# Attention and routed experts on one core: normalising two slots behind a batch's scores, turning and product three, ScalarE's copies ahead of its exponentials

## The reference

```python
def xattn(x, latents):             # 128 batches, 64 rows of 128 each
    xn, ln = _layernorm(x, gamma_m, beta_m), _layernorm(latents, gamma_l, beta_l)
    q = (ln @ Wq + bq) * DH ** -0.5            # 8 heads of 128
    k, v = split(concat([xn, ln], 1) @ Wkv + bkv)
    out = softmax(q @ k.T) @ v                 # per head, 64 x 128 scores
    return out @ Wo + bo
def ffn(x):                        # 8 experts, the best 2 of each row
    probs = softmax(x @ Wr + br)
    cw = probs where among its row's top 2, else 0
    h = relu(x @ W1[e] + b1[e])                # 128 -> 256
    return sum_e cw[e] * (h @ W2[e] + b2[e])   # 256 -> 128
x = x + tanh(g_xattn) * xattn(ctx, _layernorm(x))
x = x + tanh(g_ffn) * ffn(_layernorm(x))
```

## Time and profile before

| | us |
|---|---|
| runs | 794.71, 795.09, 797.86 |
| median | 795.09 |
| profiled execution, its own time | 800.09 |
| its span, first to last instruction | 798.37 |
| first scores (batch 0) | 29.13 |
| last scores (batch 127) | 681.25 |

### The profile page before, as it was taken

One profiled execution on the slowest core, in us unless ns is written; L12 is line 12 of the kernel. 1 busy time (PEld: TensorE's weight loads), 2 busy tenths in 40 slices (PEclk: granted clock), 3 DMA queues, 4 the chain that ended last, 5 costly groups with the idle time before them and its releaser, 6 DMA issues.

```text
span 798.4 us, 17460 instructions
## 1 busy us (share of the span) xinstructions
PE 761.3 (95%) x5392; PEld 645.5 (81%) x5392; DVE 525.9 (66%) x1829; ACT 497.8 (62%) x1630; POOL 443.1 (55%) x455
## 2 busy tenths in 40 slices
PE   7999999999999999999999999999999999879788
PEld 7778777777888988788988788988878889768665
DVE  4636677685857567677658777767768556465536
ACT  3677767676866566766556576656568655445622
POOL 2233264646552444785656686565668465466663
PEclk9999999999999999999999999999999999999999
DMA  6745151542455542174654146575316456534523
GB/s 196 199 161 193 59 210 71 210 145 81 145 186 158 200 153 71 41 231 160 214 195 146 47 109 219 189 230 172 104 44 199 146 191 205 162 107 122 149 77 87
DMA packets 119791, 119.42 MB, mean 150 GB/s; under 512 B 14585, under 2 KB 94994, under 8 KB 119698
## 3 DMA queue, kind: packets, MB, share of 16 engines
q1 hardware_dynamic: 111088, 102.41, 39.0%
q0 software_dynamic: 7680, 15.74, 6.7%
q10 hardware_dynamic: 930, 0.15, 0.1%
HBM read 35.94 MB, written 41.55 MB: 97 GB/s over the span
## 4 chain that ended last, share of the span: by engine, by line
PE 79%; DVE 6%; issue 6%; ACT 4%; POOL 2%; another core or an unknown queue 2%; DMA 1%; SPq 1%; ACTq 0%; DVEq 0%; POOLq 0%
PE shared L1426 14%; PE batch L1364 12%; PE batch L1377 12%; PE hid_ps L1294 8%; PE xy_ps L1308 7%; PE batch L1372 6%; PE shared L1217 3%; PE shared L1219 3%; PE shared L1218 3%; PE batch L1308 2%; ACT probs L746 2%; PE xy_ps L1271 2%; PE batch L1354 1%; PE shared L1415 1%
## 5 line engine op out<-in xcount | busy, mean ns | idle before, releaser
L676 POOL TENSOR_TENSOR probs<-probs,rsums 128x512 f32<-128x512 f32 x128 | 132.9, 1038 | 234.3 <-DVE rsums L1147 232.0
L746 ACT ACTIVATE probs<-batch,neg_max 128x128 f32<-128x128 f32 x512 | 180.5, 374 | 2.0 <-DVE neg_max L1151 2.0
L651 POOL DMA_INDIRECT sorted_x<-xn,row_of x120 | 121.3, 1011 | 36.0 <-issue 28.0
L827 ACT ACTIVATE qT<-shared,tb 128x512 f32<-128x512 f32 x128 | 87.2, 696 | 85.4 <-PE shared L1219 75.8
L1377 PE MATMUL batch<-pT_sb,kvn 128*128 128x512 f32 x256 | 134.2, 606 | 5.5 <-ACT pT_sb L754 5.4
L1364 PE MATMUL batch<-kvT,qT 128*128 128x128 f32 x1024 | 135.4, 275 | 0.8 <-ACT qT L827 0.8
L1426 PE MATMUL shared<-M,oT 128*128 128x128 f32 x1024 | 125.3, 275 | 0.2
L1364 PEld LDWEIGHTS batch<-kvT,qT 128*128 128x128 f32 x1024 | 124.4, 192 | 1.2 <-ACT qT L827 1.2
L1426 PEld LDWEIGHTS shared<-M,oT 128*128 128x128 f32 x1024 | 119.5, 192 | 1.3 <-issue 1.3
L746 ACT ACTIVATION_READ_ACCUMULATOR probs<-batch,neg_max 128x1 f32 x512 | 110.3, 215 | 0.0
L761 ACT ACTIVATE oT<-batch 128x512 f32<-128x512 f32 x128 | 76.2, 595 | 47.6 <-PE batch L1377 42.6
(11 more groups left out here) (168 smaller groups left out, 1241.7 us busy)
## 6 DMA issues: line engine op xcount, KB each, us to landing
wt<-wall SPq DMA_DIRECT2D x124, 321.0 KB
sorted_x<-yg SPq DMA_DIRECT2D x36, 512.0 KB, 4.9
xt<-sorted_x SPq DMA_DIRECT2D x162, 64.0 KB
sorted_y<-y_sb SPq DMA_DIRECT2D x78, 128.0 KB
kv<-in_ctx_dram SPq DMA_DIRECT2D x16, 256.0 KB
kv<-in_x_dram SPq DMA_DIRECT2D x16, 256.0 KB
xres<-in_x_dram SPq DMA_DIRECT2D x32, 128.0 KB
out_dram<-x SPq DMA_DIRECT2D x15, 256.0 KB
```

Of the source, the lines that this page charges most:

```text
L651: nc.gpsimd.indirect_dma_start(xs[k % SETS][:, :], bass.IndirectOffsetOnAxis(ap=row_of[:, g, choice, c:c + 1], axis=0), xn[:, g % 2, c, :] ...
L676: nc.gpsimd.tensor_tensor(pv, pv, rsums[:, m % 2, :].unsqueeze(2).broadcast_to([P, 4, P]), ALU.mult).then_inc(probs_ready, 1)
L746: last = nc.scalar.activation(probs[:, m % 2, c * P:(c + 1) * P], batch_ps[m % BANKS][:, c * P:(c + 1) * P], ACT.Exp, bias=neg_max[:, m % ...
L827: nc.scalar.activation(qT[:, g % 2, :, number, :], sh[:, :].rearrange("p (b i) -> p b i", b=GB), ACT.Identity, bias=tb[:, number:number + ...
```

## The change

The reciprocal and the multiply of batch m move from slot m + 1 to m + 2 (`REST`), turning and the product from m + 2 to m + 3. ScalarE copies the turned probabilities ahead of the slot's exponentials and no longer behind them. Turning and product go into the bank that the scores of batch m + 1 had (`later_ps`), so that turning also waits for that batch's exponentials, and scores wait for the copy of batch m - 5 instead of m - 4. On TensorE scores come ahead of turning, but for the first slot of a group. What hangs on a group's products, or is numbered like it, comes one slot later: the projection, the second layer norm, routing, scatters, gathers, tiles, the dense expert, and also the load and the layer norm of the next group's rows and their turning. The queries keep their last slot, so that they lie in slots 4 to 7 instead of 3 to 7. `TAIL` becomes 132. The diff shows two of the nine VectorE steps whose slot number goes up by one; the others, and the router's exponential on ScalarE (6 to 7), change in the same way. No instruction on data is added or taken away.

```diff
-LOAD = -15
-STATS = (-12, -12)
-AGGREGATE = -11
-NORMALISE = (-9, -9, -8, -8)
+LOAD = -14
+STATS = (-11, -11)
+AGGREGATE = -10
+NORMALISE = (-8, -8, -7, -7)
...
-EXP, TURN, OUT = 1, 2, 2
+EXP, REST, TURN, OUT = 1, 2, 3, 3
...
-SCATTER = (2, 3, 4, 6)
+SCATTER = (3, 4, 5, 7)
...
-HOMES = 4
-
-MEASURE = {7:(0,1),1:(2,),2:(3,)}
+HOMES = 5
+
+MEASURE = {0: (0, 1), 2: (2,), 3: (3,)}
...
-        n = max(n, GB * (LAST_GROUP[k] + 2) + 7 + AHEAD)
+        n = max(n, GB * (LAST_GROUP[k] + 2) + 8 + AHEAD)
...
-GATHERS = {0: 2, 1: 2, 5: 2, 7: 2}
+GATHERS = {0: 2, 1: 2, 2: 2, 6: 2}
...
-BIAS_SLOT = GB * (G + 1) + 2
+BIAS_SLOT = GB * (G + 1) + 3
 
 SHARED = {
-    0: [("project", -1, 2, "a"), ("place", -2, 0, "c")],
-    1: [("turn_kv", 1, 0, "a"), ("turn_kv", 1, 1, "b")],
-    2: [("project", -1, 3, "a"), ("table", -2, 0, "c")],
-    3: [("query", 1, 0, "a"), ("query", 1, 1, "b")],
-    4: [("project", 0, 0, "a"), ("turn_x", -1, 0, "b"), ("query", 1, 2, "c")],
-    5: [("router", -1, 0, "a"), ("query", 1, 3, "b"), ("query", 1, 4, "c")],
-    6: [("project", 0, 1, "a"), ("query", 1, 5, "b")],
-    7: [("query", 1, 6, "a"), ("query", 1, 7, "b")],
+    1: [("project", -1, 2, "a"), ("turn_kv", 1, 0, "b"), ("place", -2, 0, "c")],
+    2: [("turn_kv", 1, 1, "a")],
+    3: [("project", -1, 3, "a"), ("table", -2, 0, "c")],
+    4: [("query", 1, 0, "a"), ("query", 1, 1, "b"), ("query", 1, 2, "c")],
+    5: [("project", 0, 0, "a"), ("turn_x", -1, 0, "b"), ("query", 1, 3, "c")],
+    6: [("router", -1, 0, "a"), ("query", 1, 4, "b"), ("query", 1, 5, "c")],
+    7: [("project", 0, 1, "a"), ("query", 1, 6, "b"), ("query", 1, 7, "b")],
 }
...
+        def later_ps(m):
+
+            return batch_ps[(m + 1) % BANKS]
+
...
@@ def _(sp)
-                    g = (n + 1 - 4 * half) // GB
-                    if s == (7, 3)[half] and 0 <= g < G:
+                    g = n // GB
+                    if s == (0, 4)[half] and 0 <= g < G:
...
@@ def _(pool)
-                m = n - EXP
+                m = n - REST
...
-                    if s == (1, 7)[half] and 0 <= g < G:
+                    if s == (2, 7)[half] and 0 <= g < G:
...
-                if s == 2 and 0 <= g < G:
+                if s == 3 and 0 <= g < G:
...
@@ def _(act)
-                nc.scalar.activation(pT_sb[:, :], batch_ps[m % BANKS][:, :], ACT.Copy).then_inc(pT_done, 1)
+                nc.scalar.activation(pT_sb[:, :], later_ps(m)[:, :], ACT.Copy).then_inc(pT_done, 1)
...
             def slot(n):
                 if 0 <= n - OUT - 1 < B:
                     keep_product(n - OUT - 1)
+                if 0 <= n - TURN < B:
+                    keep_turned(n - TURN)
                 if 0 <= n - EXP < B:
                     exponentials(n - EXP)
-                if 0 <= n - TURN < B:
-                    keep_turned(n - TURN)
...
@@ def read_logits(n, s)
-                if s == 5 and 0 <= g < G:
+                if s == 6 and 0 <= g < G:
...
@@ def _(pe)
-                wait(pe, o_out, m - BANKS + 1)
+                wait(pe, o_out, m - BANKS)
...
             def turn_probs(m):
                 pe.wait_ge(probs_ready, m + 1)
+                if m + 1 < B:
+                    pe.wait_ge(exp_done, m + 2)
+                else:
+                    pe.wait_ge(o_out, m - BANKS + 1)
                 for c in range(4):
-                    last = nc.tensor.transpose(batch_ps[m % BANKS][:, c * P:(c + 1) * P], probs[:, m % 2, c * P:(c + 1) * P], ident[:, :])
+                    last = nc.tensor.transpose(later_ps(m)[:, c * P:(c + 1) * P], probs[:, m % 2, c * P:(c + 1) * P], ident[:, :])
...
             def slot(n):
                 if n >= TAIL and n + 1 in TILE_AT:
                     turn_tile(TILE_AT[n + 1])
+                if 0 <= n < B and n % GB:
+                    scores(n)
                 if 0 <= n - TURN < B:
                     turn_probs(n - TURN)
-                if 0 <= n < B:
+                if 0 <= n < B and n % GB == 0:
                     scores(n)
```

More of the change, by code:

```diff
@@ L760, in keep_product @@
                     wait_shared(act, shared_full, "project", g - 1, b // 2)
-                nc.scalar.activation(oT[:, :, b * L:(b + 1) * L], batch_ps[m % BANKS][:, :].rearrange("p (h i) -> p h i", h=H),
+                nc.scalar.activation(oT[:, :, b * L:(b + 1) * L], later_ps(m)[:, :].rearrange("p (h i) -> p h i", h=H),
                                      ACT.Copy).then_inc(o_out, 1)
@@ L766, in slot @@
                     keep_product(n - OUT - 1)
+                if 0 <= n - TURN < B:
+                    keep_turned(n - TURN)
                 if 0 <= n - EXP < B:
                     exponentials(n - EXP)
-                if 0 <= n - TURN < B:
-                    keep_turned(n - TURN)
                 g = n // GB - 1
-                if n % GB == 6 and 0 <= g < G:
+                if n % GB == 7 and 0 <= g < G:
                     act.wait_ge(route_step, ROUTE * g + 2)
@@ L839, in weights @@
             def weights(n):
-                if n == NORMALISE[0]:
+                if n == FOLD_FROM:
                     dve.wait_ge(got_small, 16 * 4)
@@ L947, in normalise_rows @@
                 g = n // GB - 1
-                if s == 3 and 0 <= g < G:
+                if s == 4 and 0 <= g < G:
                     dve.wait_ge(rstd1_done, g + 1)
@@ L992, in rank_experts @@
                 g = n // GB - 1
-                if s == 6 and 0 <= g < G:
+                if s == 7 and 0 <= g < G:
                     dve.wait_ge(rexp_done, g + 1)
@@ L1025, in count_rows @@
                 g = n // GB - 2
-                if s == 1 and 0 <= g < SORTED:
+                if s == 2 and 0 <= g < SORTED:
                     k = CHUNK_OF_GROUP[g]
@@ L1057, in list_tiles @@
                 g = n // GB - 2
-                if s == 1 and 0 <= g < SORTED and g == LAST_GROUP[CHUNK_OF_GROUP[g]]:
+                if s == 2 and 0 <= g < SORTED and g == LAST_GROUP[CHUNK_OF_GROUP[g]]:
                     k = CHUNK_OF_GROUP[g]
@@ L1097, in keep_table @@
                 g = n // GB - 2
-                if s == 3 and g in LAST_GROUP:
+                if s == 4 and g in LAST_GROUP:
                     k = CHUNK_OF_GROUP[g]
@@ L1376, in product @@
                 pe.wait_ge(pT_done, m + 1)
-                nc.tensor.matmul(batch_ps[m % BANKS][:, :], kvn[:, m % KVN, :], pT_sb[:, :], start=True, stop=True).then_inc(o_ready, 1)
+                nc.tensor.matmul(later_ps(m)[:, :], kvn[:, m % KVN, :], pT_sb[:, :], start=True, stop=True).then_inc(o_ready, 1)
             def slot(n):
```

## The result

| | before | after |
|---|---|---|
| median of 4 runs, us | 796.47 | 808.94 |
| lowest to highest | 794.71 to 797.86 | 807.59 to 809.78 |
| profiled execution, its span | 800.09, 798.37 | 809.66, 807.93 |
| first scores, last scores | 29.13, 681.25 | 29.60, 685.63 |

The ratio is 1.0155 (95% interval 1.0131 to 1.0178): slower by 1.6%. The forecast was 788, in a range of 780 to 798.

What follows compares the result with a forecast made beforehand. TensorE's work was taken to bound the kernel wherever tiles run, with 21.8 us lost elsewhere. From 795.09 us, -21.8 + 11.6 + 0.5 + 2.5 = -7.2 gave 787.9, said as 788.0, range 780 to 798.

Steps and rivals of the forecast that it cites:

- TensorE's work sets the pace wherever tiles run: Groups full of tiles: 48.60 us against 48.5 of work, nothing lost, so the change neither gains nor costs there.
- Copies ahead of exponentials: ScalarE's order: product waits about 0.9 us after turning; without tiles 0.45 us lost in slot 2, 0.6 in slot 4.
- Scatters move with their readers: Scatters and gathers on SP's and GpSimd's queues move along with their readers and keep their distance, at no cost.
- Turning's wait goes: Between 30 and 205 us, turning's 11.0 us of waiting for GpSimd's multiply goes.
- A stretch keeps 1.65: Each of seven stretches without tiles still loses 0.1 + 0.45 + 0.6 + 0.5 = 1.65 us.
- 0.5 for normalising drawn out by GpSimd: VectorE's normalising of the next kv in slots 0 and 1, slowed by GpSimd's multiply, costs 0.5 us a group.
- The rule on the shared ports: VectorE and GpSimd hold shared ports in turn for a whole instruction; by it the sum would be 3.5 us worse.
- The start: Group 0: first scores 0.5 us later, first product 3.7 later; costs 2.0 us, 2.5 with the 0.5.
- a sign of being wrong: A granted clock of 0.50 between 30 and 45 us would show the prediction wrong.
- its rival with a chance of 0.10: TensorE's waits around the first turning drop its clock to half: 1.7 us more, 789.6 us; chance 0.10.
- The end: Drain after the last batches: everything moves one slot later together, costing nothing if work paces those slots.
- the case on the other side: VectorE becomes the bound beside tiles, about 1.8 us a group in eight groups' worth: 802.3 us; chance 0.13.

Runs made afterwards that it cites:

- e5: Kernel after, with turning ahead of the scores on TensorE in every slot but the second of a group: 795.99 us, ratio 0.9992.
- e9: e5, with GpSimd's second scattering transfer held behind ScalarE's copy of the turned tile in slots 3 and 7: 794.94 us, ratio 0.9954.

## Why the prediction was wrong

The steps that failed are those that cost the tile groups nothing: "TensorE's work sets the pace wherever tiles run, and that this change can earn only where they do not". From a group that lost nothing I concluded that it could lose nothing. The parts with tiles (slots 40 to 47, the full groups, the stretches) missed the forecast by 12.9 us (7.6 measured, -5.3 said). Their lost time was 13.6 us before, 21.2 in after, 15.8 in e5 and 11.3 in e9, so that two edits show where most of it is.

- *Copies ahead of exponentials.* The product's cover was counted ("In slots with a projection (1.79) or a tile (0.89 and more) TensorE has work for that time"), but not the next tile's copy, which stands behind the exponentials on ScalarE, nor who waits for it in the same slot, the output. And the change's "On TensorE scores come ahead of turning", with its 0.89 us ahead of all of ScalarE's slot, was costed at nothing. Turning's place alone (e5) takes back 5.4 of the 12.9, and 4.1 more in slots 8 to 39.
- *Scatters move with their readers*: "DMAs keep their distance". They moved from slots 2 and 6 to 3 and 7, as the projections did, but not in time: GpSimd's multiply no longer waits for exponentials of its own slot, and the transfers behind it come earlier in the slot. In slot 2 of before's tile group the second was issued at 394.05, 0.49 us behind the start of the projection's last matmul (393.56), and VectorE's and ScalarE's reads were in time; timeline of before:

```profile
393.88 0.35 DVE L1172 SCALAR_TENSOR_TENSOR x<-shared,tg,xres 128x128 f32<-128x128 f32 x1
394.05 0.97 POOL L651 DMA_INDIRECT sorted_x<-xn,row_of  x1 [0.30 <-issue]
394.09 0.38 ACT L783 ACTIVATE xtT<-xy_ps 128x256 f32<-128x256 f32 x1 [2.50 <-PE xy_ps L1271]
```

  In slot 3 of after and of e5 it is issued 0.58 us ahead of that matmul and lies over the ends of the projection and of the turned tile. Moving it behind the copy (e9) takes back 4.5.

The remaining 3 lie in the stretches, whose slots without tiles keep waits of 0.2 to 0.6 us in e9 too. The other steps:

- *Turning's wait goes*: right, 0.2 of 11.0 us is left between 30 and 205 us.
- *A stretch keeps 1.65*: the group without tiles kept 2.2 (34.73 less the work of 32.5). By slots: 0.12 in slot 0 (0.1 said), 0.60 in slot 2 (0.45), 0.70 in slot 4 (0.6), and about 0.3 each in slots 3, 5 and 7, not foreseen.
- *0.5 for normalising drawn out by GpSimd*: wrong. In the group without tiles the two steps took 2.3 us for 8 instructions each, where the first of them took 3.6 for 9 before; groups by line of after and of before:

```profile
L901 DVE SCALAR_TENSOR_TENSOR kv<-kv,mv,gamma 128x128 f32<-128x128 f32 x8 | 2.3, 344 | 0.0
```

```profile
L898 DVE SCALAR_TENSOR_TENSOR kv<-kv,mv,gamma 128x128 f32<-128x128 f32 x9 | 3.6, 451 | 0.0
```

  The move took them away from GpSimd's add, and the multiply fell elsewhere. The rule on the shared ports was not tested by that.
- *The start*: the first product came 3.4 us later (39.82; 3.7 said), the group lost 1.6 (2.0 said): right. Its 0.5 ahead of the scores is less than what executions differ by there. But the clock did fall in after's profiled execution, a sign of being wrong by the prediction and its rival with a chance of 0.10; window of after, columns as in the earlier trace rows:

```profile
32.50:35.90 3.40, 3.40 (x17) 3.40 (x17) 3.21 (x14) 1.35 (x7) 0.00 (x0) 0.50 0.00 0
```

  TensorE had been busy from 29.60 on, behind a wait of 0.78 us, so it fell ahead of the waits that the rival named. In e5 it fell there as well (0.50 from 33.7 us), in e9, whose order differs from e5's only in slots with tiles, it did not, and group 0 took 30.58 and 30.37 us: 0.2, where the rival had 1.7. What it cost in after's own order no run tells apart.
- *The end*: 0 said, +1.9 measured between the two profiles, open as told.
- *The rivals*: the case on the other side came true in sign (7.2 us slower there, 12.5 measured), but not by VectorE, busy 32.63 of 50.09 us there; it was ScalarE's queue and GpSimd's transfers that held TensorE. The chance for slower was 0.13, since only one engine had been tried for that part.

## What to carry to other kernels

A stage that loses nothing is no stage that can lose nothing: when a step moves in an engine's queue, follow each instruction that now stands behind it to its reader, in the stages that lost nothing as well. Two results in one bank make such a reader; then the order on the producing engine, here turning ahead of the scores, is worth more than the order on the copying one. And when a group runs at exactly its work, look for the reads that a new order would put near the end of an issue of GpSimd's indirect transfers.

## What the hardware showed that was not expected

Reads of TensorE's results were late near the end of GpSimd's issue of an indirect transfer. Take a read of a projection, turned tile, turning, scores, output or turned kv, with the reader idle, that begins over 0.55 us after the start of the last matmul: between 30 and 690 us the trace of after has 39, all with such an issue between matmul and read, e5 27 (25), e9 20 (16); before had 10 (7). In after they came 0.3 to 1.1 us behind the usual 0.3.

Most reads near an issue are in time all the same. Count the reads whose engine was free 0.3 us after the last matmul's start, when they were due: in after 31 of the 72 that were due 0.6 to 1.5 us after the start of an issue were late, 3 of the 36 due earlier in it, and none of the 240 others. The load of the DMA engines alone does not do it: it was 0.92 in e5's slot 3 and 0.97 in e9's, where the reads were in time.

In the drain of before the stretch without a matmul looks the same: turning was issued at 690.22, and its copy began behind two gathers, as did VectorE's next read; timeline of before:

```profile
690.73 0.94 POOL L666 DMA_INDIRECT yg<-sorted_y,home  x1 [0.31 <-issue]
...
691.98 0.94 POOL L666 DMA_INDIRECT yg<-sorted_y,home  x1 [0.30 <-issue]
693.94 0.60 ACT L754 ACTIVATE pT_sb<-batch 128x512 f32<-128x512 f32 x1 [3.94 <-remote]
694.03 0.69 DVE L1158 TENSOR_TENSOR hs<-hid_ps,wt 128x512 f32<-128x512 f32 x1 [2.60 <-remote]
```

By the trace's semaphore events TensorE's signals for these two reads came at 693.92 and 694.01, 0.02 us ahead of them, though the last matmuls had been issued at 690.59 and 691.64: the readers were not slow. e9 shows that moving one transfer takes the lateness away at its place; no run moved one in the drain. Whether the signal is late or the matmul's end, and whether the issue or the transfer does it, was not told apart. The Trainium skill ("Perfetto Trace Analysis", section "Summary: the profiler window per engine type") says that the row of a transfer from GpSimd ends with its descriptors and not with its data, and that TensorE's end in the profile is an estimate. That a read began 0.7 us after the transfer's row had ended (391.70 to 392.43 in e5) fits it; no run here shows where the data ends.
